# A four-layer gated transformer on one core: the third attention's keys and folded keys made in the second attention's tail, norms 3 and 4 interleaved, scores in plain fp32, softmax in halves

## The reference

```python
    x = x + tanh(g_xattn[1]) * _L1_xattn_ref(_layernorm(x), ctx, ...)   # 32 heads of 16
    x = x + tanh(g_ffn[1])   * _L1_ffn_ref(_layernorm(x), base_W, gate_W, lora_A, lora_B)  # 28 experts, top 2
    x = x + tanh(g_xattn[2]) * _L2_xattn_ref(_layernorm(x), ctx, Wq, bq, Wk, bk)
    x = x + tanh(g_ffn[2])   * _L2_ffn_ref(_layernorm(x), w1, w2, w3)   # gated, NF4 weights
```

## Time and profile before

| | us |
|---|---|
| median of 3 runs | 1685.16 |
| lowest and highest run | 1682.34, 1685.91 |
| profiled execution, its own time | 1684.98 |
| span of the profile | 1683.2 |

### The profile page before, as it was taken

One profiled execution on the slowest core, in us unless ns is written; L12 is line 12 of the kernel. 1 busy time (PEld: TensorE's weight loads), 2 busy tenths in 40 slices (PEclk: granted clock), 3 DMA queues, 4 the chain that ended last, 5 costly groups with the idle time before them and its releaser, 6 DMA issues.

```text
span 1683.2 us, 18435 instructions
## 1 busy us (share of the span) xinstructions
PE 1413.8 (84%) x6556; PEld 1000.1 (59%) x6556; DVE 1173.3 (70%) x1817; ACT 608.2 (36%) x913; POOL 360.6 (21%) x403
## 2 busy tenths in 40 slices
PE   6999999998988878887888887999999999994104
PEld 5665555664665565665666665677777777763001
DVE  4899999988888977434444446566566666676777
ACT  3556555564224424202211122344444434432003
POOL 1112222122270203121011102122222212225400
PEclk9999999999999989856999999899999999997557
DMA  5699999999300012531011301011011101000001
GB/s 195 173 222 218 214 211 214 225 206 186 122 24 1 1 37 52 125 79 38 21 37 37 104 26 38 26 38 63 29 54 44 64 26 38 1 1 1 0 0 50
DMA packets 40129, 136.36 MB, mean 81 GB/s; under 512 B 5184, under 2 KB 11200, under 8 KB 33840
## 3 DMA queue, kind: packets, MB, share of 16 engines
q0 software_dynamic: 13824, 51.91, 16.6%
q1 hardware_dynamic: 26224, 83.38, 14.8%
HBM read 72.63 MB, written 10.75 MB: 50 GB/s over the span
## 4 chain that ended last, share of the span: by engine, by line
PE 53%; DVE 24%; DMA 10%; DVEq 5%; issue 3%; ACT 3%; SPq 0%; POOL 0%; ACTq 0%
PE PS L151 11%; PE PS L153 10%; PE PS L152 10%; DMA AR<-AR 10%; PE PS L882 4%; PE PS L918 4%; DVE AR L651 3%; DVE AR L2274 2%; DVE AR L2268 2%; DVE AR L2272 2%; PE PS L904 2%; DVE X L2010 2%; DVEq L343 1%; DVEq L334 1%; DVE s_sb L346 1%
## 5 line engine op out<-in xcount | busy, mean ns | idle before, releaser
L424 POOL DMA_DIRECT2D AR<-AR x92 | 92.6, 1054 | 325.4 <-DMA AR<-AR 137.5
L521 PE MATMUL PS<-R,PT 128*128 128x512 f32 x256 | 125.8, 637 | 21.1 <-DVE X L686 21.1
L152 PE MATMUL PS<-R16r 128*128 128x512 f32 (+1 forms) x328 | 122.6, 374 | 0.0
L153 PE MATMUL PS<-R16r 128*128 128x512 f32 (+1 forms) x312 | 120.2, 385 | 0.0
L496 PE MATMUL PS<-R,HT 128*128 128x256 f32 x512 | 115.9, 379 | 0.0
L496 PEld LDWEIGHTS PS<-R,HT 128*128 128x128 f32 x512 | 94.8, 190 | 11.6
L521 PEld LDWEIGHTS PS<-R,PT 128*128 128x128 f32 x256 | 50.3, 203 | 84.2 <-issue 83.5
L151 PE MATMUL PS<-R16r,HTr 128*128 128x512 f32 (+1 forms) x224 | 89.9, 402 | 3.9 <-DVE X L1287 2.5
L151 PE MATMUL PS<-HTr,R16r 128*128 128x512 f32 (+1 forms) x240 | 90.3, 376 | 3.1 <-DVE R16r L184 1.6
L1018 ACT COPY AR<-PS 128x512 f32<-128x512 f32 x64 | 37.5, 586 | 144.6 <-PE PS L153 144.2
L153 PE MATMUL PS<-HTr,R16r 128*128 128x512 f32 (+1 forms) x240 | 87.7, 365 | 0.0
(11 more groups left out here) (305 smaller groups left out, 3541.6 us busy)
## 6 DMA issues: line engine op xcount, KB each, us to landing
AR<-AR POOLq DMA_DIRECT2D x92, 528.0 KB, 6.3
OR<-in_wo SPq DMA_DIRECT2D x12, 1024.0 KB, 7.8
dequantised<-AR SPq DMA_DIRECT2D x8, 1056.0 KB, 5.4
WR<-in_w0q SPq DMA_DIRECT2D x8, 1024.0 KB, 9.4
AR<-in_w3q SPq DMA_DIRECT2D x8, 1024.0 KB, 4.9
WR<-dequantised SPq DMA_DIRECT2D x22, 256.0 KB, 2.8
AR<-in_nf SPq DMA_DIRECT2D x4, 1056.0 KB, 7.1
nf_in<-in_nf SPq DMA_DIRECT2D x4, 1056.0 KB, 6.9
```

The costliest lines, as they stand in the source:

```text
L152: nc.tensor.matmul(out, ah, bl, start=False, stop=False)
L153: return nc.tensor.matmul(out, al, bh, start=False, stop=last_)
L424: nc.gpsimd.dma_start(nf_below(g)[:, part], what[:, part], accum_op=ALU.add, max_dma_last_dim=4 * N_NF // 2).then_inc(added, 16)
L521: i = nc.tensor.matmul(bank(5 + tt), PT[:, at:at + P], vo[:, pr, b, :], start=pr == 0, stop=pr == 1)
```

## The change

- The keys' 16 matmuls go to `pe_a1`, four behind each of its last four steps, into bank 1; their bias copies to ScalarE's queue there and at the start of `act_f1`. The query weights get a place of their own (WQ2) and are loaded early.
- Norm 3 uses banks 2 and 3: tiles 0 and 1 are turned within step 15, tiles 2 and 3 scaled before the last additions, and `logits` of each tile runs behind the transposes of the tile two on. The expert weights' high parts are cast at steps 8 and 9 instead of 9 and 10.
- Folded keys and bias row stand between the logits and four (not three) base products. The hidden values are turned two tiles ahead. Six tiles of norm 4 are scaled and turned within the last three spreads.
- Norm 4 is kept in plain fp32 (HT0, M2): no high and low parts, five plain matmuls a score tile. The softmax, its transposes and copies go in two halves of four tiles.
- The turns of gated block 0 and the first two of block 1 stand within the third attention, the third of block 1 behind tile 3 of norm 5. `pe_f2_turn`, `act_f2_high`, `dve_f2_low` are the old loop bodies made functions.
- Late group: rise 6 in the expert stage, mask 4 within the softmax, rise 7 and mask 5 behind norm 5; POOL scales blocks 0 and 1 between the pairs of norm 4; SP loads blocks 2 to 5 ahead of the group's store.

```diff
-        NORM_BANKS = {0: (5, 6), 1: (0, 1), 3: (0, 1), 4: (0, 1), 5: (4, 7), 6: (5, 6)}
+        NORM_BANKS = {0: (5, 6), 1: (0, 1), 3: (2, 3), 4: (0, 1), 5: (4, 7), 6: (5, 6)}
...
+        PLAIN = (0, 4, 7)
+
+        def lows(n):
+            return T * sum(k not in PLAIN for k in range(n))
+
         def norm_low(dve, n, t):
-            if n == 0:
+            if n in PLAIN:
...
-                pe.wait_ge(lo_ready, T * (n - 1) + t - 1)
+                pe.wait_ge(hi_ready if n in PLAIN else lo_ready, T * n + t - 1 if n in PLAIN else lows(n) + t - 1)
...
-                nc.scalar.copy((HT0 if n in (0, 7) else HTh)[:, :, t * P:(t + 1) * P],
+                nc.scalar.copy((HT0 if n in PLAIN else HTh)[:, :, t * P:(t + 1) * P],
...
+                if u == NU - 1:
+                    pe_norm_tile(pe, 3, 0)
+                    pe_norm_tile(pe, 3, 1)
                 weigh(u)
                 if u + 3 < NU:
                     scores(u + 3)
+                if u >= NU - C:
+                    pe_a2_keys(pe, u - NU + C)
...
+        def pe_a2_keys(pe, dc):
+            if dc == 0:
+                pe.wait_ge(A2["k_in"], 16)
+                pe.wait_ge(A1["qT_ready"], 2 * B)
+            if dc == 2:
+                pe.wait_ge(A2["kt_ready"], 2)
+            for c in range(C):
+                i = nc.tensor.matmul(k2_bank(dc), WR[:, c * D + dc * P:c * D + (dc + 1) * P], CT[:, c, :],
+                                     start=c == 0, stop=c == C - 1)
+            i.then_inc(A2["k_mm"], 1)
...
-                if u == 9:
+                if u == NU - 2:
+                    act_a2_keys(act, 0)
+                    act_a2_keys(act, 1)
+                if u == 8:
                     act.wait_ge(F1["w_in"], 16)
                     act.wait_ge(A1["q_mm"], 2 * B)
                     nc.scalar.copy(Wh[:, 0:C * NWF // 2], WR[:, 0:C * NWF // 2])
-                if u == 10:
+                if u == 9:
...
+        def act_a2_keys(act, dc):
+            act.wait_ge(A2["k_mm"], dc // 2 * 2 + 2)
+            nc.scalar.activation(KT2[:, dc * 256:(dc + 1) * 256], k2_bank(dc), ACT.Identity,
+                                 bias=b2[:, C + dc:C + dc + 1]).then_inc(A2["kt_ready"], 1)
...
+                    norm_scaled(dve, 3, 0)
+                    norm_scaled(dve, 3, 1)
...
+            norm_low(dve, 3, 0)
+            norm_scaled(dve, 3, 2)
+            norm_low(dve, 3, 1)
+            norm_scaled(dve, 3, 3)
             add(B - 1, 0)
             add(B - 1, 1)
+            dve_stats(dve, PAIRS - 1)
...
+            sp.dma_start(WR[:, 0:2048], l2k_d).then_inc(A2["k_in"], 16)
+            sp.wait_ge(A1["s_mm"], NU)
+            sp.dma_start(WQ2, l2q_d).then_inc(A2["q_in"], 16)
...
+            accumulate(pool, LATE, 1)
+            accumulate(pool, LATE, 2)
+            pool_norm_pair(pool, 4, 0)
+            accumulate(pool, LATE, 3)
+            pool_norm_pair(pool, 4, 1)
+            pool_f2(pool, (0, 1))
+            pool_norm_pair(pool, 4, 2)
+            pool_norm_pair(pool, 4, 3)
+            accumulate(pool, LATE, 4)
+            pool_norm(pool, 5)
+            accumulate(pool, LATE, 5)
+            join(pool, LATE)
+            pool_f2(pool, range(2, NF))
...
+            pe_norm(pe, 3, logits, 2)
+
+            def folded_keys():
+                pe.wait_ge(A1["acc"], 2 * B)
+                pe.wait_ge(A2["kt_ready"], C)
+                pe.wait_ge(A2["q_in"], 16)
+                for ic in range(C):
+                    for dc in range(C):
+                        nc.tensor.matmul(bank(ic // 2)[:, (ic % 2) * 256:(ic % 2 + 1) * 256],
+                                         WQ2[:, dc * D + ic * P:dc * D + (ic + 1) * P],
+                                         KT2[:, dc * 256:(dc + 1) * 256], start=dc == 0, stop=dc == C - 1)
+                pe.wait_ge(F1["lg_ready"], T - 1)
+                for dc in range(C):
+                    i = nc.tensor.matmul(bank(6)[0:1, 0:256], b2[:, dc:dc + 1], KT2[:, dc * 256:(dc + 1) * 256],
+                                         start=dc == 0, stop=dc == C - 1)
+                i.then_inc(A2["m_mm"], 1)
...
+            folded_keys()
+            for t in range(4):
+                base(t)
+            pe.wait_ge(F1["h_ready"], 1)
+            pe.wait_ge(F1["lg_ready"], T)
+            pe.wait_ge(A2["m_ready"], 1)
+            turn_h(0)
+            turn_h(1)
+            pe.wait_ge(F1["b_in"], 16)
+            for t in range(T):
+                spread(t)
+                if 0 < t < 5:
+                    base(t + 3)
+                if t + 2 < T:
+                    turn_h(t + 2)
+                if t > 4:
+                    pe_norm_tile(pe, 4, 2 * t - 10)
+                    pe_norm_tile(pe, 4, 2 * t - 9)
...
+            act.wait_ge(A2["m_mm"], 1)
+            nc.scalar.copy(BK, bank(6)[0:1, 0:256])
+            nc.scalar.copy(M2, bank(0, 2)).then_inc(A2["m_ready"], 1)
...
+                elif t == 4:
+                    norm_scaled(dve, 4, 0)
+                    norm_scaled(dve, 4, 1)
+                    up(dve, LATE, 6)
+                elif t == 5:
+                    norm_scaled(dve, 4, 2)
+                    norm_scaled(dve, 4, 3)
+                elif t == 6:
+                    norm_scaled(dve, 4, 4)
+                    norm_scaled(dve, 4, 5)
+            dve_stats(dve, PAIRS - 1)
...
+        KT2 = WR[:, 2048:2048 + C * B * SK]
+        WQ2 = R16[:, 14336:16384]
+        M2 = OT[:, 0:C * B * SK]
+        BK = s_sb[0:1, 1, 0:B * SK]
+
+        def half2(h):
+            return s_sb[:, 0, h * 256:(h + 1) * 256]
+
+        def scores2(h):
+            return bank(4 if h else 7)[:, 0:4 * SK]
...
+                    pe.wait_ge(F1["acc"], T)
+                pe.wait_ge(hi_ready, T * 4 + t + 1)
                 tok = slice(t * P, (t + 1) * P)
-                o = bank(7)[:, t * SK:(t + 1) * SK]
+                o = scores2(t // 4)[:, t % 4 * SK:(t % 4 + 1) * SK]
                 b = t // 2
                 nc.tensor.matmul(o, ones[0:1, :], BK[:, b * SK:(b + 1) * SK], start=True, stop=False)
                 for c in range(C):
                     m = slice(c * 256 + b * SK, c * 256 + (b + 1) * SK)
-                    i = mm3(o, HTh[:, c, tok], HTl[:, c, tok], OTh[:, m], OTl[:, m], False, c == C - 1)
+                    i = nc.tensor.matmul(o, HT0[:, c, tok], M2[:, m], start=False, stop=c == C - 1)
                 i.then_inc(A2["s_mm"], 1)
-            pe_norm(pe, 4, scores)
-            pe.wait_ge(A2["probs"], 1)
+
+            def turn_p(h):
+                pe.wait_ge(A2["probs"], h + 1)
+                for t in range(4):
+                    i = nc.tensor.transpose(bank(2 + h)[0:SK, t * P:(t + 1) * P], half2(h)[:, t * SK:(t + 1) * SK], ident[:])
+                i.then_inc(A2["t_mm"], 1)
+
+            def outputs(h):
+                pe.wait_ge(A2["pt_ready"], h + 1)
+                pe.wait_ge(A2["b_in"], 16)
+                for t in range(4 * h, 4 * h + 4):
+                    if t >= 2:
+                        pe.wait_ge(A2["acc"], t - 1)
+                    b = t // 2
+                    nc.tensor.matmul(bank(t % 2), PT[0:SK, t * P:(t + 1) * P], CB[:, b * D:(b + 1) * D],
+                                     start=True, stop=True).then_inc(A2["mm"], 1)
+            for t in range(6):
+                scores(t)
+            pe_f2_turn(pe, 0, 0, 0)
+            pe_f2_turn(pe, 0, 0, 1)
+            pe_norm_tile(pe, 4, 6)
+            pe_norm_tile(pe, 4, 7)
+            scores(6)
+            scores(7)
+            pe_f2_turn(pe, 0, 0, 2)
+            turn_p(0)
+            outputs(0)
+            turn_p(1)
+            outputs(1)
...
+        def act_a2(act):
+            def exps(h):
+                act.wait_ge(A2["shifted"], h + 1)
+                nc.scalar.activation(half2(h), half2(h), ACT.Exp, scale=float(D) ** -0.5).then_inc(A2["exps"], 1)
+
+            def probs(h):
+                act.wait_ge(A2["t_mm"], h + 1)
+                nc.scalar.copy(PT[0:SK, h * 512:(h + 1) * 512], bank(2 + h)[0:SK, :]).then_inc(A2["pt_ready"], 1)
+            exps(0)
+            act_f2_high(act, 0, 0, 0)
+            act_f2_high(act, 0, 0, 1)
+            act_norm(act, 4, (6, 7))
+            act_f2_high(act, 0, 0, 2)
+            probs(0)
+            exps(1)
+            probs(1)
...
+            shift(0)
+            norm_scaled(dve, 4, 6)
+            norm_scaled(dve, 4, 7)
+            dve_f2_low(dve, 0, 0, 0)
+            dve_f2_low(dve, 0, 0, 1)
+            norm(0)
+            dve_f2_low(dve, 0, 0, 2)
+            shift(1)
+            down(dve, LATE, 4)
+            norm(1)
...
+            sp.wait_ge(A2["m_mm"], 1)
             load(1, 1)
+            sp.wait_ge(F1["t_mm"], T)
+            sp.dma_start(CB, ctxB_d.rearrange("k b n -> k (b n)")).then_inc(A2["b_in"], 16)
...
+            pe_f2_turn(pe, 1, 1, 0)
+            pe_f2_turn(pe, 1, 1, 1)
             pe.wait_ge(A2["acc"], T)
-            turn_w(0, 0, True)
-            turn_w(1, 1)
-
```

(40 more changed lines are left out.)

198 lines of the change are left out of this document (73 added, 125 removed).

## The result

The changed kernel takes **1645.03 us** (median of four runs, 1641.86 to 1648.69) against 1683.75 (four runs, 1681.27 to 1685.91) on the same chip: a ratio of **0.9771**, 95% interval 0.9745 to 0.9797, or 38.7 us less. The forecast was 1647 and the range 1630 to 1662. The profiled execution took 1644.17 us, its span is 1642.4.

A forecast was written before the change was run, and what follows sets the result against it. Bound: VectorE's pace to 603, TensorE mostly busy to 681, then one stage after another, mostly at half clock from 701. Terms +1.6 - 35.6 + 2.9 - 6.5 = -37.6 from 1685.0 gave 1647.4 us; range 1630 to 1662.

The forecast's parts named there:

- Keys in the tail: Second attention's tail: 3.4 of the keys' 7.2 us show; its last output product ends at 613.5.
- Norm 3, expert stage: Norm 3 to the expert stage's last addition: 14.9 us to last logits at 628.4, routing 644.4, end 683.0, +1.6.
- The stall: Expert stage: VectorE's scaling of tiles 4 and 5 waits for POOL's third pair, 2 us, bounded by 0 and 6.
- S to the outputs: From S, the expert stage's last addition, to the third attention's first output: 27.1 us, -35.6.
- rival 2: Third attention's scores: plain products dear at 64 columns too, 1.3 times three fp32r ones; 1659 us, chance 0.05.
- The four passes: Score products: true fp32 takes four array passes, so each would be a third dearer than three fp32r products.
- 20 us for eight tiles: Third attention's scores: 2.5 us a tile at half clock, 20 us for eight (18.4 to 24.8).
- Outputs: Third attention's first output to its last addition: 17.8 us with a wait for VectorE, +2.9.
- To the first product: From the third attention's last addition to the end of the gated feed-forward's first block product: 31.2 us, -6.5.
- Rival 1: Third attention: the clock stays high, 1628 us; a fall in the middle about 1636; chance 0.23 throughout or for part.
- rival 3: Changed stretch: in-order queues cost 13 us more (POOL wait, all keys showing, handings over); 1660, up to 1670; chance 0.10.
- rival 4: Gated loop: half clock lasts into it, each block grows by some 18 us; chance 0.05.

The follow-up runs named there:

- keys_back: The changed kernel with the keys' matmuls and bias copies put back from the second attention's tail to ahead of the folded keys; 1650.82 us, ratio 0.9811.
- before_warm: The kernel before, fp32r products kept, with 13 unread wide products filling TensorE's wait ahead of norm 4; 1680.14 us, ratio 0.9983.
- turns_back: The changed kernel with all six turns of gated blocks 0 and 1 put back behind the third attention's last addition; 1647.5 us, ratio 0.9788.
- whole_softmax: The changed kernel with both halves' probabilities turned ahead of any output of the third attention; 1644.31 us, ratio 0.9768.
- ordered: The changed kernel reordered only: gated turns and norm 4 tiles 6, 7 singly between score tiles, POOL scaling split, mask and second half's turn moved; 1630.64 us, ratio 0.970.
- pool_early: The changed kernel with POOL's scaling of gated blocks 0 and 1 moved ahead, behind the late group's first accumulate; 1638.18 us, ratio 0.9724.
- pool_split: The changed kernel with POOL scaling gated block 0 early, in the routing, and block 1 behind norm 4's third pair; 1640.17 us, ratio 0.975.
- warm_hole: The changed kernel with ten unread wide products added behind the expert stage's last spread, where TensorE waits; 1640.48 us, one run.
- plain_hole: The kernel before with plain norm 4, folded keys and scores, and the folded keys' subtraction kept, unread, so the hole stays; 1664.16 us, one run.
- before_plain: The kernel before with only norm 4, folded keys and score products made plain fp32; 1662.33 us, ratio 0.9866.
- plain_hole_timed: The same kernel as plain_hole, timed in six runs against the kernel before; 1665.79 us, ratio 0.991.

## Why the prediction was right

Step by step, on the axis of the profiled executions:

- **Keys in the tail.** Forecast: the last output product ends at 613.5, 3.4 of the keys' 7.2 us show. Measured: its addition begins at 612.6, so 2.4 show. keys_back puts the whole part's worth at 6 us.
- **Norm 3, expert stage.** Last logits at 628.4 forecast, 627.0 measured; routing 644.4 against 642.5. The terms written for the logits do not add up to the 14.9: eight groups of 1.4 and eight tiles of 0.5 are 15.2 alone, and only six tiles' transposes were still to come. **The stall was mis-sized**: 2 us taken within 0 to 6, and 3.62 measured. The working counted POOL's two blocks at 6.2 us; they took 6.96 (672.28 to 679.24). POOL came to them late besides: the second pair's two small operations, with the wait between them, took 7.0 us (665.34 to 672.31, much of it beside VectorE's rises), where the third pair's took 1.1. How the 3.62 divide between the two is not shown. What the working also left out, that VectorE is slowed beside POOL's scaling (L201: 2.28 instead of 0.99), cost nothing in this place, since VectorE stood waiting behind it. The routing, 1.9 earlier than forecast, paid for the stall: S at 682.2 against 683.0.
- **S to the outputs.** Forecast 27.1, measured 24.3: the largest miss. The price of a tile was right (2.5 forecast, 2.51 measured at half clock), and rival 2, plain products dearer at 64 columns too, is ruled out: an fp32r tile took 3.20 us at half clock in the kernel before (705.99 to 709.19) and 1.72 at full in before_warm, a plain one 2.51 and 1.39. The four passes that the forecast weighed against this decide nothing at 64 columns. **What failed was the term "20 us for eight tiles", which kept the clock low throughout**: it came back at 701.6, so tiles 6 and 7 took 1.39 each, 2.2 less, and the third turn and the first half's transposes ran at full clock too. In turns_back and whole_softmax it did not come back there, so this miss is partly chance: the low clock that the forecast assumed is what a second execution can give.
- **Outputs.** 17.8 forecast and measured; the wait for VectorE was there (2.42 us) where it was put.
- **To the first product.** 31.2 forecast, 31.1 measured.
- **Sum.** At P: +0.8 - 38.5 + 2.9 - 6.5 = -41.3, where -37.6 was forecast; behind it +0.5, so -40.8 between the profiled executions, and by medians -38.7. The median came out 2 us below the forecast. The profiled pair, which the working is about, missed it by 3.2, so 1 us or so of the nearness is luck.

The largest term, S to the outputs, was not undone by itself in the changed kernel: no run puts its folded keys back or gives it fp32r scores. What it owes to the moved keys and folded keys is read from the two timelines.

Rival 1 was the one to take more seriously. The clock was high for 7 of the 42 us from S to A (701.6 to 708.4), the weak form of it, and again from 742.5, with the first wide products, as forecast. The reason given for its strong form (TensorE fed without a hole) is only half of what decides. The argument against it, that 64-column products keep the clock low, lumped two kinds together: between transposes plain ones held it in all three profiles taken and in the times of most runs, fp32r ones in none. Of rival 3 a part of the longer stall occurred, and nothing showed of the rest; rival 4 did not occur, the loop kept its length.

The same error shows in what the change leaves unused. In the kernel before, plain products alone gave 21.8 us, with each tile's transposes beside its scores. The change made six tiles' transposes earlier and so issued six tiles of bare 64-column products, behind a hole of its own making; there the six tiles gained only the plain form's price, 6 x 0.69 = 4.1 us. It paid anyway because 21 us of keys, folded keys and hole between S and norm 4's first tile (681.4 to 702.4) were gone. ordered has both.

Left open: what in the products makes the chip keep or lower the clock. The runs show only which orders did; plain products without transposes lost it (pool_early, pool_split, warm_hole), the fp32r order was profiled twice, and the moment of a fall or a rise varied between executions of the same order.

## What to carry to other kernels

Price a stage of narrow products at both clock levels, and look in the trace for what kind of work each level went with; then move a stage's transposes and turns between its narrow products rather than ahead of them. When a helper engine shares a memory port with the pacing one, its work has two prices, what waits for it and what it slows, and moving it may only exchange them. Time a run that hangs on the clock several times: one profile (plain_hole) looked like certainty and was four cases of six.

## What the runs showed of the hardware that was not expected

- Eight 64-column plain tiles between transposes ran at a granted clock of 1.00 from 698 to 714 (before_plain); with fp32r ones between the same transposes it fell to 0.50 at 706.5, 3.5 us after the last idle time (before_warm). The Trainium skill (TensorE: Matmul & The Clock Gate, HAM oscillation) puts a lost clock down to idle gaps. Here it was lost with TensorE busy around the fall (before_warm, pool_early at 688.0 with TensorE busy since 679), so the measurement decides: gaps are not the only cause. Through a gap of 3.07 us it was kept in both profiles of the plain form (plain_hole, plain_hole_timed) and lost in the kernel before.
- At 64 columns one plain fp32 product is cheaper than three fp32r ones: 1.39 against 1.72 us a tile at full clock, 2.51 against 3.20 at half.
- Eight small VectorE operations (128 x 224) took 5.07 us instead of 2.50 while POOL scaled a block.
